# Moving the zeroing of a scatter table in HBM from beside a sort to beside a build of a count matrix

## The reference

```python
edge_index = jnp.stack([src, dst])
x = _layernorm(x + _L0_gnn_ref(x, edge_index, 4), axis=-1)   # four hops of normalised neighbour sums
x = _layernorm(x + _L1_gnn_ref(x, src, dst, ...), axis=-1)   # an MLP per edge, sum and maximum per target
x = _layernorm(x + _L2_gnn_ref(x, edge_index, ...), axis=-1) # three convolutions
x = _layernorm(x + _L3_gnn_ref(x, relation_emb, edge_index, edge_type_33), axis=-1)  # hyperbolic messages, two hops
return x
```

## Time and profile before

| | us |
|---|---|
| median of 3 runs (5718.3 to 5719.78) | 5718.8 |
| the profiled execution's own time | 5712.27 |
| its span, first to last instruction | 5710.5 |
| sort, from its first clear to the next stage's first operation | 38.5 to 133.4 |
| build of the count matrix, first to last operation | 274.5 to 739 |

### The profile page before, as it was taken

How to read it: one execution, slowest core, us unless ns; L and a number is a source line. 1 busy time by engine, 2 the same in 40 slices (tenths; PEclk the granted TensorE clock), 3 DMA queues, 4 the chain that set the end, 5 groups by cost and what they waited for, 6 DMA issues and landing times. The chain is left out here.

```text
span 5710.5 us, 76336 instructions
## 1 busy us (share of the span) xinstructions
PE 2917.1 (51%) x18212; PEld 2314.5 (41%) x18213; DVE 3715.3 (65%) x6539; ACT 1759.2 (31%) x5177; POOL 3453.4 (60%) x3383
## 2 busy tenths in 40 slices
PE   4344578724555555264736426455564244555543
PEld 1233456514454444143424225444453234444443
DVE  4645554306777777233332569899998579998987
ACT  0055500001111111110010035655654146556552
POOL 4077337737777777432613477777772577777771
PEclk7655589956666666566857655556655556665655
DMA  6031040027777777500000212222220321222211
GB/s 214 31 106 52 0 142 2 2 79 205 217 214 221 214 216 203 173 9 0 4 7 9 53 42 58 45 54 50 50 46 7 68 54 44 55 49 50 53 32 18
DMA packets 491952, 449.20 MB, mean 79 GB/s; under 512 B 135374, under 2 KB 439172, under 8 KB 491667
## 3 DMA queue, kind: packets, MB, share of 16 engines
q1 hardware_dynamic: 257963, 232.05, 14.7%
q0 software_dynamic: 116768, 136.51, 10.3%
q10 hardware_dynamic: 116936, 77.08, 4.2%
HBM read 308.22 MB, written 137.16 MB: 78 GB/s over the span
## 5 line engine op out<-in xcount | busy, mean ns | idle before, releaser
L2158 POOL DMA_INDIRECT tg<-tab_d,tail_ids x1632 | 1699.1, 1041 | 543.3 <-issue 494.6
L445 POOL DMA_INDIRECT sorted_edges_d<-place_batch x784 | 807.9, 1030 | 749.6 <-DMA place_batch<-place_queue_d 340.0
L2197 PE MATMUL acc<-msg,sum_hot 128*96 128x65 f32 x3264 | 547.0, 366 | 961.0 <-ACT msg L2271 748.5
L2197 PEld LDWEIGHTS acc<-msg,sum_hot 128*96 128x96 f32 x3264 | 529.4, 279 | 976.9 <-issue 976.9
L1494 POOL DMA_INDIRECT xg<-tab_d,src_i x784 | 767.7, 979 | 252.3 <-issue 238.5
L2187 PE MATMUL hr<-near_table,near_hot 128*128 x4896 | 679.2, 266 | 197.2 <-DVE near_hot L2319 95.0
L2187 PEld LDWEIGHTS hr<-near_table,near_hot 128*128 128x128 f16 x4896 | 497.4, 105 | 380.5 <-issue 281.8
L2246 ACT ACTIVATE pr<-hr 128x396 f32<-128x396 f32 x576 | 277.8, 483 | 590.9 <-PE hr L2187 584.7
L2260 ACT ACTIVATE msg<-tg,coef_b 128x64 f32<-128x64 f32 x1632 | 396.6, 334 | 31.3 <-DVEq L2667 31.3
L1508 PE MATMUL hq<-ex,sameU 128*128 128x128 f32 x1568 | 269.2, 350 | 260.5 <-DVEq L1613 194.4
L2487 DVE TENSOR_REDUCE scal<-prod 128x17 f32<-128x1088 f32 x288 | 370.5, 1286 | 9.9
(11 more groups left out here) (469 smaller groups left out, 5402.5 us busy)
## 6 DMA issues: line engine op xcount, KB each, us to landing
ex<-spread_d SPq DMA_DIRECT2D x112, 448.0 KB, 5.5
msg_d<-back ACTq DMA_DIRECT2D x112, 448.0 KB
near_hot<-head_row_d SPq DMA_DIRECT2D x96, 408.0 KB
tg<-tab_d,tail_ids POOLq DMA_INDIRECT x1632
spread_d<-zeros ACTq DMA_DIRECT2D x28, 896.0 KB, 10.9
spread_d<-zeros SPq DMA_DIRECT2D x28, 896.0 KB, 8.8
idsU<-dst_short_d SPq DMA_DIRECT2D x112, 224.0 KB, 6.6
pairs_d<-pair_m SPq DMA_DIRECT2D x3, 4800.0 KB
```

The costliest lines, as they stand in the source:

```text
L445: l.eng.indirect_dma_start(K.sorted_edges[:, :], bass.IndirectOffsetOnAxis(ap=K.batch[:, n % 2, 0, k:k + 1], axis=0), K.batch[:, n % 2, 1, ...
L2158: e.indirect_dma_start(tg[:, u % TAILS * GQ + k, :], None, K.tab3, bass.IndirectOffsetOnAxis(ap=K.tail_ids[:, u * GQ + k:u * GQ + k + 1], ...
L2197: ins = e.matmul(sums[:, bass.ds(at[k], D + 1)], sum_hot[u % 2][:, k, :], msg[u % QN][:, k, :], start=False, stop=False, skip_group_check= ...
```

## The change

ScalarE's program is taken out of the sort, so no clear is issued there. In the build SP issues clears n x 7 to n x 7 + 6 behind the load of batch n, for all n from 0 to 7. The total stays 56. Nothing else changes.

```diff
-        def scalar(l):
-            for n in range(STEPS // 2):
-                clear_rows(l, K, K.spread1, n)
-
         def tensor(l):
...
-        drive(nc, "places", dict(sync=sync, vector=vector, gpsimd=gpsimd, scalar=scalar, tensor=tensor))
+        drive(nc, "places", dict(sync=sync, vector=vector, gpsimd=gpsimd, tensor=tensor))
...
         def sync(l):
             for n in range(8):
                 queue_batches(l, K, n, 1)
-                for step in range(STEPS // 2 + n * 4, min(STEPS // 2 + n * 4 + 4, STEPS)):
+                for step in range(n * STEPS // 8, (n + 1) * STEPS // 8):
                     clear_rows(l, K, K.spread1, step)
```

## The result

The changed kernel takes **5728.12 us** (median of 19 runs, 5715.76 to 5732.87) where the kernel before, run beside it, takes 5716.48 (19 runs, 5702.82 to 5719.78). The ratio is **1.0021 [1.0014, 1.0028]**, +11.6 us. The forecast was 5741, a move of +22. The time lies in the forecast's range, the direction is right, and the move is about half of what was forecast.

The account below looks back on a forecast made before the run. The build's closed chain of rounds, slowed by clears, and the sort's end were taken to bound the kernel. -3 us at the sort's end and +25 in the build gave +22 on 5718.8: 5741 us, range 5726 to 5754.

Parts of the forecast that it names:

- What bounds the build: Build: rounds are a chain without slack, each burst of four clears loses about 3.8 us, by reading through slow register loads.
- Part 1: Sort's end: without its 28 clears the store of `place_i` ends sooner, -3 us (bounds 0 and -8).
- its other bound, -8: Sort's end: 8 us saved if the lag from 126 us on was also left by the clears.
- Part 2: Build: seven clears behind each of eight batch loads, at 0.96 us a clear (0.72 in the first two bursts), +25.4 us.
- six more: 4.3: Build's first two bursts, run together: 8 clears become 14, six more at 0.72 us each, +4.3 us (0 to 5.8).
- rival B: Build: bursts of seven choke at 205 GB/s from the fifth clear with rounds still slow; +39, 5758 us; chance 0.10.
- rival A: Build: loss belongs to a burst's start, not its length; only the eighth burst adds, +3.8; 5720 us; chance 0.11.
- 0.82 for "above 5730.2 us": Whole kernel: chance 0.82 given to a slowdown of over 0.2%, that is a time above 5730.2 us.
- low bound's 2.2 and 5.0 us: Build: less-than-linear case if loss leans on a burst's start, 5 x 2.2 + 5.0 + 0 = +16 us.
- Rival C: Sort's end was all clears, -11.3 us, and added clears cost under 0.2 us each; 5707.5 us; chance 0.04.
- Part 3: Build: later batch loads behind seven clears, about 18 us of a 45 us batch, and a later GpSimd cost nothing.

Follow-up runs that it names:

- doubled loads: Kernel before, with TensorE loading each round's nine register values from SBUF twice: 7728.17 us beside 7613.91 (one run each).
- late burst: Kernel before, with the build's 28 clears sent in one burst after the last scatter: 7629.34 us beside 7613.91 (one run each).
- second profile: The changed kernel run again without any edit, against the kernel before: 5740.7 us (5 runs), ratio 1.0037.
- early burst: Kernel before, with the build's 28 clears in one burst behind the second batch load, beside scatters: 5708.9 us against 5714.06.

## Why the prediction was right and wrong

- **What bounds the build** (the rounds are a closed chain; the clears slow them): held. That clears slow them by reading SBUF is shown by the source of the zeros. That it is TensorE's register loads that come late was called a reading and remains one, with the longer slow rounds under doubled loads for it and the unchanged loss of a burst against it.
- **Part 1, -3 us, was mis-sized: -5.7 to -6.3.** In every kernel without clears at the sort's end the next stage starts at 126.5 to 127.8 us, against 131.7 to 133.4 with them. I took only the engine time of the clears' own queue (3.0 us) and left the tail from 126 us on standing. The tail was the clears' too: it went with them. The step had named this as its other bound, -8, and the value lies nearer to that. This miss of some 3 us is in every profile.
- **Part 2, the price of 0.96 us a clear, held where the rate is full.** Bursts six to eight lose 7.2 to 7.4 us, 1.03 to 1.06 a clear (forecast 6.7 to 6.8, so a little too low); the late burst without scatters 1.03; the second profile of the changed kernel +26.1 in all (forecast +25.4). As totals, against the build with no slow round: 23.1 + 2.4 = 25.5 us for 28 clears before, 0.91 each; 51.6 for 56 in the second profile, 0.92; 44.7 for 56 in the first, **0.80**.
- **The failed step is the term of part 2 for the first three bursts**, 0.72 us a clear for the first two and 0.96 for the third, carried over to a longer burst. In the profile of the result, the first two bursts cost 7.1 us, not 10.0 (5.7 before and the "six more: 4.3"), and the third 3.1, not 7.1. These three are 6.9 us below the forecast; the fourth and fifth are 0.95 below it and the last three 1.85 above. They cost less because the rate fell beside the scatters. I had seen the low rate in the earlier trace rows, and priced it in rival B as the *worst* case, clears lasting longer with rounds just as slow. The runs show the reverse: in stretches at 222 to 246 GB/s a round is nearly its own length. The earlier trace rows already held the hint, the round of 2.70 us from 297.61 with clears in flight; I used it only as a sign for rival A. In the second profile the same three bursts lose 15.0 us in place of 17.1, so there the term is off by 2 us and not by 7; why the low rate lasts is not known.
- **The base.** 2.3 us of the miss is no fault of a step: the kernel before came out at 5716.48, not 5718.8. The account: -3.3 (part 1), -6.2 (part 2), +3.1 (rest of the span), -4.4 (medians move less than the two profiles: 11.6 against 16.0), -2.3 (base) = -13.1, counted from 5718.8 + 22.4 = 5741.2, which the forecast gave as 5741. The +3.1 and the -4.4 have no cause shown: the sum put nothing behind the build, and the profiles lie where they lie among runs that spread over 17 us.
- **What was luck.** The time lies only 2 us inside the low end of the range, and 3.1 us behind the build, of unknown cause, helped it there. The 0.82 for "above 5730.2 us" went to times that the median of 5728.12 doesn't reach. The low bound's 2.2 and 5.0 us had no row behind them; the fourth burst did grow by 2.2.
- **Rival A** (a burst has a fixed loss): ruled out by four slow rounds in each of the bursts four to eight and by one clear per turn, which costs 0.62 us without a burst. **Rival B** (long bursts choke with slow rounds): its sign came, a stretch of full engines over 25 us in one burst of seven (the third, from 325 to 355 us), but not its price: that burst is the cheapest. The late burst shows rounds slow for 65 us, but at full rate, so at the linear price. **Rival C** (faster): part of its ground, the sort's end, was half right (-6 of its -11), but the 28 clears more cost 19.2 us, 0.69 each, far over its 0.2.
- **Part 3** (nothing from what is moved past): held. The second batch load went out at 278.44 us behind seven clears, and in the build GpSimd waited 2.3 us in all for a batch, as before (2.4). Its "about 18 us" of full engines for seven clears held for the later bursts; the third took 30, and the first two 53 together, until just before the third.
- By the rule that the Trainium skill's page "DMA: Bandwidth & Descriptors" gives under "Rules for kernel authors", a DMA issued early and waited for late overlaps with compute (its words are that "the fixed setup cost overlaps"; of what the transfer does to the compute beside it the row says nothing). For clears out of SBUF the runs disagree, by 0.8 to 0.9 us a clear, and for clears out of HBM on the faster chip they agree (no slow round).

**What stays open.** What makes the low rate last until the third burst in one profile of the changed kernel and end near 311 us in another: both ran the same program, where the kernel before takes 5716 and 5714 us, and I found nothing in the queues ahead of it. Whether it is TensorE's register loads, or something else without a record, that clears out of SBUF hold up. Why the slow chips have slow rounds beside scatters alone. A build without clears never ran on a chip of the first kind.

## What to carry to other kernels

Ask of a "free" background DMA where it reads: bulk transfers out of SBUF slowed a loop in which TensorE loads its registers from SBUF, with no semaphore between them, and a source in HBM cured it on the faster chip (5682 us, 32 under the kernel before). Where a price per transfer comes from one stretch, look at the rate beside it before it is carried to a stretch at another rate; here full engines meant a round of 4.7 us on average at over 330 GB/s and of 3.5 at 150 to 250. And when bulk traffic stands ahead of a small store that ends a stage, count the tail of the transfer to the traffic, not only its queue's own busy time.

## What the hardware did that I had not expected

- **Full engines, two rates.** Clears alone ran at 373 GB/s (share 1.03) with GpSimd idle. Beside scatters, in the early burst, the engines moved 241 to 245 (share 1.07 to 1.10), and 400 again when these ended.
- **The source decides.** The rounds were slowed by clears that read SBUF (3.81 us at 250 to 330 GB/s, 17 rounds), and not by clears that read HBM (3.03, 11 rounds), on the faster chips.
- **A small store behind bulk.** The store of 392 KB in small pieces landed 13.9 us after its issue with clears ahead of it and 8.1 without.
- **Chips of two speeds.** The same kernel took 5714 us on one chip and 7520 to 7614 on five others. In the profiles of 5712 and 7622 us the build differs by 18 us; the rest is lost in later stages. In the build slow rounds stand beside the scatters with no clears near them. The two kernels with longer turns, one clear per turn (6.52 us) and the doubled loads (7.70), had few or none of these extra slow rounds. I have no cause for either.
